# All work behind six transformer layers recast as ten stages that begin inside the layers' last four steps

## The chip, the cores and the metric

The kernel runs on one core of one Trainium2 chip. Its time is the device time of one execution in microseconds (us). TensorE is called PE, VectorE DVE, ScalarE ACT, GpSimd POOL and SyncE SP.

## What is computed

The input is `x`, 8 samples of 512 tokens with 128 channels, all in fp32. Four blocks follow one another, and each stands in `x = x + layernorm(block(layernorm(x)))`:

```python
# 1: six layers of linear attention with a feed-forward part (leaky relu)
for i in range(6):
    xn = _layernorm(x, ln1_w[i], ln1_b[i])
    q, k, v = xn @ wq[i], xn @ wk[i], xn @ wv[i]          # 8 heads of 16
    x = linear_attn(softmax(q, -1), softmax(k, -2), v) @ wo[i] + bo[i] + x
    xn = _layernorm(x, ln2_w[i], ln2_b[i])
    x = leaky_relu(xn @ w1[i]) @ w2[i] + x                # 128 -> 512 -> 128
# 2: spiking network
h = square(relu(x @ W_fc.T)); y = h @ W_proj.T            # 128 -> 512 -> 128
# five steps of a leaky integrator; the result is how often it fires / 5
# 3: state space model: u = x @ Win.T + bin; y = irfft(rfft(u) * rfft(k)) + u * D
y = y @ Wout.T + bout
# 4: gated channel mix with the token before
r = sigmoid(xr @ W_r.T); out = r * (square(relu(xk @ W_k.T)) @ W_v.T)
```

## The kernel before, in words

Each engine has one hand-written queue of instructions, with semaphores between them (`then_inc` where something is done, `wait_ge` where it is needed). A sample is 128 partitions x 512 columns, and nearly every instruction works on such a tile or on its four 128-column parts. An "item" is one sample in one layer, 48 in all (`ITEMS`). The program goes by steps: in step n every engine does some part of item n (attention), n-1 (the output projection), n-2 (second norm, `second_scale`, `second_turn`, `second_copy`, `second_low`) and n-3 (the feed-forward part, PE's `h` and `y`, ACT's `hl`). Steps 0 to 50 are the `layers` steps, and within each the order of an engine's instructions is the order of the lines in its function `step`.

The work behind the layers has stages of its own: ADD, PART, TURN, FFN, SPIKE, STATE, CONV, BACK, SHIFT, GATE, FINISH are numbered 0 to 10, and sample v is in stage k at step 48 + k + v. Steps 51 to 65 stand in a second function on each engine, `late_step`. The spiking network's first two matrix products go through the layers' own functions and buffers: its input is normalised with the layers' `STATS`, `JOIN` and `RSTD`, turned and split into a high and a low f32r part (`X2H`, `X2L`), and multiplied as three f32r matmuls (`split3`) with `FCH` and `FCL`. POOL's `join` and `ln1_power` serve both the layers and these samples.

What comes behind it is one chain for each sample: `count` adds five thresholded tiles on PE (`SPK`); four normalisations, each with DVE's `stats` (four `bn_stats`, four `bn_aggr`), POOL's `rstd` or `rstd_mean` (a power of -0.5 and two small products), ACT's `normalise` or `scaled` and POOL's addition to `X` (L778); `bands`, `transform`, `products`, `inverse`, `back_bands` and `project_out` for the convolution; `key_and_gate` and `value` for the last block. PSUM has eight banks, PS0 to PS7: `pXT`, `pQ`, `pK`, `pX2`, two of `pH`, `pY` and `pW`, and who writes one waits until the last reader is through.

In `late_step` PE does, in this order: `project_in`, the spiking products with `inverse` between them, `key_and_gate`, `second_turn`, `count`, `transform`, `value`, `project_out`, the turns. DVE has `products` at the very end of a step, and `inverse`, which needs them, comes in the next.

Of the kernel before, what the change touches and what calls it, by code (L numbers as in the profile page):

```python
# [13 lines left out]
P = 128  # L14
# [15 lines left out]
ALL = ITEMS + BATCH  # L30
# [54 lines left out]
def layers(step):  # L85

    for n in range(ITEMS + 3):
# [10 lines left out]
def live(n):  # L100

    return n < ITEMS, 1 <= n <= ITEMS, 2 <= n < ALL + 2, 3 <= n < ALL + 3

ADD, PART, TURN, FFN, SPIKE, STATE, CONV, BACK, SHIFT, GATE, FINISH = range(11)


def sample(n, stage):

    v = n - ITEMS - stage
    return v if 0 <= v < BATCH else None


def passed(n, stage):

    return max(0, min(BATCH, n - ITEMS - stage + 1))


def late(step):  # L120
    for n in range(ITEMS + 3, ITEMS + BATCH + FINISH):
        step(n)
# [3 lines left out]
DECAY = BATCH  # L126
# [4 lines left out]
SPECTRUM = {ITEMS: (0, 1, 2, 3), ITEMS + 1: (4, 5, 6, 7), ITEMS + 2: (8,)}  # L131
# [7 lines left out]
def build(nc, x, qkv, wo, w1, w2, lnc, bo, fcT, proj, winT, woutT, alog, bmat, cmat, dtr, dp, bins_,  # L139
          bouts, wrT, wkT, wvT, mu, ident, cent, hmask, iota, fwd, fwdx, inv, out):  # L140
    ctx = ExitStack()
    with ctx:  # L142
# [3 lines left out]
        def sem(name):  # L146
# [34 lines left out]
        MVS = [sb(f"MV{i}", [8]) for i in range(5)]  # L181
        STS = [sb(f"ST{i}", [24]) for i in range(5)]
        VES, RS, NMS = ([sb(f"{n}{i}", [4]) for i in range(5)] for n in ("VE", "R", "NM"))
# [21 lines left out]
        YM, ACC, MEM, U = QF, QB, EK, EKT  # L205
# [23 lines left out]

        PS = [ctx.enter_context(nc.psum_tensor(f"PS{i}", [P, SEQ], FP32)) for i in range(8)]  # L230
# [4 lines left out]
            "bias_out bias_ps bm_out bm_ps bo_c bo_mean bo_st c_in c_ps cdb ce1 ce1_zero ct e1 e1_arg e2 e2_arg eighth "  # L235
            "ek ekT_ps ek_tm fc_hi fc_out fc_ps g_ps gt h_ps hl i_rstd i_st i_var i_ve k_fm k_out k_ps k_rec k_skip "
            "kf kf_ps kmax ktm la la_exp late_in ln1_half ln1_rstd ln2_rstd ln_part m_ps m_ready mbv mixed out_ps p_const "
            "p_part q0_in q_blk q_exp q_fm q_nrm q_ps q_rec q_sub q_sum qmax qs relu resid1 resid2 sh0 ssm_in "
            "stats_ready stored v_part w1_hi w1_lo w2_c w2_mean w2_sum w_ready win_out win_ps wo_c wo_mean wo_st "
            "wqk_hi wqk_lo wv x2T_ps x2h x2l xT_ps xTh xTl xi_init xr xr2 y_ps "  # L240
            "added ym spk cnt_ps cnt_var cnt_nm cnt_z cnt_x st_var st_rstd st_x st_T_ps st_T u_ps u_sum "
            "bands f_ps f_part spectra inv_ps second back o_ps o_sum o_var o_nm o_z o_x sh_var "
            "sh_nm sh_z sh_T_ps sh_T r_ps k2_ps r_relu r_sq r_sig v_ps rv rv_var rv_nm rv_z done").split()
# [70 lines left out]
        def _(pe):  # L314
# [44 lines left out]
            def h(item, f):  # L359
                w = item // BATCH % 2  # L360
                if f == 0:
                    if item < ITEMS:
                        pe.wait_ge(s["w1_lo"], item // BATCH + 1)
                    else:
                        pe.wait_ge(s["fc_out"], 1)
# [4 lines left out]
                high, low = (W1H[w], W1L[w]) if item < ITEMS else (FCH, FCL)  # L370
                o = slice(f * P, (f + 1) * P)
                split3(pH[f % 2][:, :], high[:, o], low[:, o], X2H[:, :], X2L[:, :]).then_inc(s["h_ps"], 1)

            def y(item, f):
                w = item // BATCH % 2
                pe.wait_ge(s["hl"], item * FB + f + 1)
                if f == 0:
                    if item < ITEMS:
                        pe.wait_ge(s["w2_c"], item // BATCH + 1)
                    if some(item):  # L380
                        pe.wait_ge(s["resid2"], min(item, ITEMS))
                    if item > ITEMS:
                        pe.wait_ge(s["ym"], item - ITEMS)
# [1155 lines left out]
```

## Time and profile before

| what | value |
| --- | --- |
| median of 3 runs | 908.49 us (907.61 to 909.62) |
| the profiled execution's own time | 908.03 us |
| its span (first to last instruction) | 906.2 us |
| PE busy in the span | 810.6 us (89%) |
| DVE busy | 667.5 us (74%) |
| ACT busy | 588.1 us (65%) |
| POOL busy | 463.3 us (51%) |
| mean granted clock of PE | 0.962 of 2.4 GHz |

The profile's times are from the span's start. Busy times count instructions that run, not waits. A row of the timeline that holds several instructions of one kind gives the time from the start of the first to the end of the last; an fp32 matmul of PE stands there as two records, so x8 is four matmuls. A matmul's own duration overlaps with the next one, so what it costs in a row of them is the distance between starts.

### The profile page before, as it was taken

The page shows a single profiled execution, that of the slowest core. Times are in us where ns is not written, and L with a number is a line of the kernel's source. Part 1 is how long each engine was busy: PE and PEld are TensorE (multiplying, and loading weights), DVE is VectorE, ACT ScalarE, POOL GpSimd, SP SyncE. Part 2 cuts the span into 40 slices and gives each one's busy share as a digit, 9 for nine tenths or more (in the row PEclk, how much of TensorE's full clock was granted, in tenths as well). Part 3 has the DMA queues.
Part 4 walks back from the last instruction along what each step waited for, and adds up shares of the span by engine and source line. Part 5 has one row for each costly group of instructions (what it writes and reads, how often), then busy time and mean ns, then how long its engine had stood idle before and what let it go on. Part 6 is the DMA issues. An engine that isn't in the chain of part 4 may idle for free. (4 is left out here: it accounts for less than half of the span.)

```text
span 906.2 us, 15899 instructions
## 1 busy us (share of the span) xinstructions
PE 810.6 (89%) x5386; PEld 707.3 (78%) x5386; DVE 667.5 (74%) x1866; ACT 588.1 (65%) x1244; POOL 463.3 (51%) x772
## 2 busy tenths in 40 slices
PE   7689999999999999999999999999689888777674
PEld 3477888998999899999999988888578776656553
DVE  4687888878778887887888878874558877587741
ACT  3476777787778777777777777656655555533353
POOL 6888446565765554454544454443453435244333
PEclk9799999999999999999999999999979998999986
DMA  8200001000010001000100000000000000000001
GB/s 256 73 1 1 1 1 37 1 1 1 1 36 2 1 1 36 1 1 1 37 1 2 1 1 1 1 2 1 1 0 1 2 0 3 11 13 13 12 12 37
DMA packets 19728, 13.70 MB, mean 15 GB/s; under 512 B 2487, under 2 KB 18494, under 8 KB 19646
## 3 DMA queue, kind: packets, MB, share of 16 engines
q1 hardware_dynamic: 19646, 12.67, 4.8%
q8 instruction: 44, 0.72, 0.4%
q14 instruction: 38, 0.31, 0.1%
HBM read 10.57 MB, written 2.10 MB: 14 GB/s over the span
## 5 line engine op out<-in xcount | busy, mean ns | idle before, releaser
L316 PE MATMUL PS<-W,HL 128*128 128x128 f32 x1536 | 201.7, 275 | 0.0
L316 PEld LDWEIGHTS PS<-W,HL 128*128 128x128 f32 x1536 | 193.2, 191 | 8.2
L888 ACT ACTIVATE HL<-PS 128x512 f32<-128x512 f32 x192 | 109.3, 593 | 18.3 <-PE PS L316 14.0
L712 POOL TENSOR_TENSOR JOIN<-STATS 128x8 f32<-128x8 f32 (+1 forms) x56 | 14.6, 262 | 197.7 <-DVE STATS L1164 197.7
L316 PE MATMUL PS<-X2H,W1L 128*128 128x512 f32 x192 | 89.3, 465 | 6.3 <-issue 5.0
L874 ACT ACTIVATE XR<-XI,RSTD 128x128 f32<-128x128 f32 x224 | 71.7, 395 | 28.5 <-POOL RSTD L730 27.9
L960 ACT ACTIVATE EK<-PS,NKM 128x512 f32<-128x512 f32 x48 | 33.0, 688 | 81.8 <-DVE NKM L1284 81.8
L1164 DVE BATCH_NORM_STATS2 STATS<-XI 128x6 f32<-128x128 f32 x384 | 82.4, 277 | 1.6 <-POOL JOIN L713 1.5
L761 POOL TENSOR_TENSOR QB<-QB,QRC 128x512 f32<-128x512 f32 x48 | 50.9, 1059 | 61.3 <-DVE QRC L1316 61.3
L316 PE MATMUL PS<-X2L,W1H 128*128 128x512 f32 x192 | 76.1, 396 | 0.0
L316 PE MATMUL PS<-X2H,W1H 128*128 128x512 f32 x192 | 75.7, 394 | 0.0
L326 PE MATMUL PS<-ID,XR 128*128 128x128 f32 x416 | 64.9, 278 | 7.9 <-ACT XR L874 7.9
L656 POOL TENSOR_SCALAR VE<-MV 128x4 f32<-128x4 f32 x40 | 8.1, 203 | 120.7 <-DVE MV L1081 119.8
L730 POOL TENSOR_TENSOR RSTD<-JOIN,MHALF 128x4 f32<-128x4 f32 x48 | 64.1, 1336 | 0.0
L316 PE MATMUL PS<-MM,QS 128*128 128x128 f32 x384 | 55.6, 289 | 4.1 <-DVE MM L1269 2.8
L723 POOL TENSOR_TENSOR RSTD<-JOIN,MHALF 128x4 f32<-128x4 f32 x56 | 56.6, 1011 | 4.4
L1291 DVE STREAM_TRANSPOSE QB<-QF 128x512 f32<-128x512 f32 x48 | 34.1, 711 | 33.1 <-ACT QF L826 33.1
L326 PEld LDWEIGHTS PS<-ID,XR 128*128 128x128 f32 x416 | 47.1, 142 | 14.2 <-ACT XR L874 12.7
L1281 DVE TENSOR_TENSOR XI<-PS,XI 128x512 f32<-128x512 f32 x48 | 33.2, 692 | 30.6 <-PE PS L316 30.6
L316 PEld LDWEIGHTS PS<-MM,QS 128*128 128x128 f32 x384 | 48.2, 197 | 8.3 <-DVE MM L1269 5.7
L316 PE MATMUL PS<-EKT,XR 128*128 128x128 f32 x384 | 51.0, 276 | 1.6 <-ACT EKT L826 1.6
L316 PE MATMUL PS<-INV,BIG 128*128 128x256 f32 x128 | 38.7, 469 | 14.6 <-DVE BIG L1366 14.6
(214 smaller groups left out, 2189.4 us busy)
## 6 DMA issues: line engine op xcount, KB each, us to landing
W<-in_w SPq DMA_DIRECT2D x12, 256.0 KB
X<-in_x SPq DMA_DIRECT2D x8, 256.0 KB, 4.9
out<-X SPq DMA_DIRECT2D x8, 256.0 KB, 2.3
QKV<-in_qkv SPq DMA_DIRECT2D x6, 192.0 KB, 2.8
FWD<-in_fwd SPq DMA_DIRECT2D x1, 1024.0 KB, 5.5
INV<-in_inv SPq DMA_DIRECT2D x1, 1024.0 KB, 8.3
WO<-in_wo SPq DMA_DIRECT2D x6, 64.0 KB
FWDX<-in_fwdx SPq DMA_DIRECT2D x1, 256.0 KB, 5.9
```

What stands on the lines that cost most here:

```text
L316: return nc.tensor.matmul(o, l, r, start=start, stop=stop, skip_group_check=True)
L326: last = nc.tensor.transpose(o[:, j * P:(j + 1) * P], i[:, j * P:(j + 1) * P], ID[:, :])
L712: pool.tensor_tensor(d, part(1), part(4), ALU.subtract)
L723: pool.tensor_tensor(RSTD[:, TILES:end], JOIN[:, 4, TILES:end], MHALF[:, TILES:end], ALU.pow).then_inc(s["ln2_rstd"], 1)
L730: power = pool.tensor_tensor(RSTD[:, 0:TILES], variance, MHALF[:, 0:TILES], ALU.pow)
L761: pool.tensor_tensor(heads(QB[:, :]), heads(QB[:, :]), QRC[:, :].unsqueeze(2).broadcast_to([P, 32, DH]), ALU.mult).then_inc(s["q_nrm"], 1)
L874: last = nc.scalar.activation(o[:, j * P:(j + 1) * P], tile(src, b, j), ACT.Copy, scale=r[:, first + j:first + j + 1])
L888: nc.scalar.activation(HL[f][:, :], pH[f % 2][:, :], ACT.Prelu, alpha=LEAK).then_inc(s["hl"], 1)
L960: nc.scalar.activation(EK[:, :], pK[:, :], ACT.Exp, bias=NKM[:, 0:1], accum_out=KSM[:, 0:1]).then_inc(s["ek"], 1)
L1164: last = nc.vector.bn_stats(STATS[:, first + j, :], tile(src, b, j))
L1281: tt(xo, pQ[:, :], xo, ALU.add).then_inc(s["resid1"], 1)
L1291: nc.vector.transpose(QB[:, :], QF[:, :]).then_inc(s["q_blk"], 1)
```

## The change

`late_step` is gone on every engine, and with it the eleven stages and the samples' way through the layers' functions. All work behind the layers is written as some fifty small operations, each of which runs on one engine for one sample in one of ten stages; sample v is in stage k at step 44 + k + v (`FIRST` is 44). The last steps of the layers (44 to 50) and the steps behind them (to 60) are the same function `step`, in which each operation stands at a given place. There are 61 steps in place of 66.

```diff
-ALL = ITEMS + BATCH
+FIRST = ITEMS - 4
...
-ADD, PART, TURN, FFN, SPIKE, STATE, CONV, BACK, SHIFT, GATE, FINISH = range(11)
...
-    v = n - ITEMS - stage
+    v = n - FIRST - stage
...
+def at(n, stage, operation, *block):
+    v = sample(n, stage)
+    if v is not None:
+        operation(v, *block)
...
-DECAY = BATCH
+DECAY = BATCH - 2
...
+STEPS_IN_ALL = FIRST + BATCH + 9
...
-        FCH, FCL = sb("FCH", [FB * P], F32R), sb("FCL", [FB * P], F32R)
+        FCC = FCT
+        X2S, X2T = sb("X2S", [SEQ]), sb("X2T", [SEQ])
...
+        YM = W2[0]
...
+        ACTS = [HA[0], HA[1], W1[0], W1[1]]
...
+            def spiking_first(v, f):
+                pe.wait_ge(s["fc_out"], 1)
+                pe.wait_ge(s["in_T"], v + 1)
+                mm(pH[f % 2][:, :], FCC[:, f * P:(f + 1) * P], X2T[:, :]).then_inc(s["fh_ps"], 1)
...
+            def spiking_second(v, f):
+                pe.wait_ge(s["fhl"], v * FB + f + 1)
+                for j in range(TILES):
+                    last = mm(pW[:, j * P:(j + 1) * P], ACTS[f][:, j * P:(j + 1) * P],
...
+                if sample(n, 6) is not None:
+                    freed("resid1", min(n-1, ITEMS))
...
+                    transform(sample(n, 6), 1)
...
+                if sample(n, 5) is not None:
+                    freed("xTh", min(n+1, ITEMS))
+                    freed("ek_tm", min(n, ITEMS))
+                    freed("cnt_z", passed(n - 1, 3))
...
+                    project_in(sample(n, 5))
...
+                    inverse(sample(n, 6))
...
+            def left_add(v):
+
+                dve.wait_ge(s["fin_rstd"], v + 1)
+                for j in range(TILES):
+                    last = stt(out=tile(X, v, j), in0=tile(XI, v, j), scalar=RS[LEFT][:, j:j + 1], in1=tile(X, v, j),
+                               op0=ALU.mult, op1=ALU.add)
...
+                at(n, 7, output_stats)
+                at(n, 6, real_products)
+                at(n, 0, left_stats)
+                at(n, 6, imaginary_products)
+                at(n, 6, spectra)
+                at(n, 5, input_bias)
+                at(n, 4, state_stats)
```

The stages are: 0 the norm behind the layers and its addition (`left_stats`, `left_add`) and the norm's numbers of the spiking input (`spiking_stats`); 1 turn, the four first products and two of the four second ones; 2 the other two; 3 spikes and count; 4 the count's norm and addition, norm and turn for the state space model; 5 `project_in`, `bands`, the first half of `transform`; 6 its second half, the products, `inverse`, `back_bands`, `project_out`; 7 two norms, an addition and a turn; 8 key, gate, value; 9 the last norm and addition. The spiking input is fp32 now and has buffers of its own, so `split3` gives way to one fp32 matmul for each f; DVE's subtraction for `X2L` and POOL's `join` and `ln1_power` fall away for these samples. `DECAY` starts the preparation of the convolution's kernel two steps earlier.

PE, one full step in the middle of the late work, before. WINC is `project_in`, PROJ and HL the spiking network's second products, INV `inverse`, SH,WK the key, WR the gate, SPK the count, FWD `transform`, WVT `value`, WOUTT `project_out`, ID a turn:

```order
L316 MATMUL PS<-WINC,BIG 128x128 x4
...
L316 MATMUL PS<-INV,BIG 128x256 x8
L316 MATMUL PS<-PROJ,HL 128x128 x4
...
L316 MATMUL PS<-SH,WK 128x512 x2
L316 MATMUL PS<-WR,SH 128x128 x8
L316 MATMUL PS<-PROJ,HL 128x128 x4
...
L316 MATMUL PS<-SPK,IDB 128x512 x5
L316 MATMUL PS<-BIG,FWD 128x128 x16
L316 MATMUL PS<-WVT,BIG 128x128 x4
L316 MATMUL PS<-WOUTT,BIG 128x128 x4
```

The same place after the change (step 52; X2T,FCT are the spiking network's first products):

```order
L317 MATMUL PS<-WINC,BIG 128x128 x4
L317 MATMUL PS<-X2T,FCT 128x512
L317 MATMUL PS<-SH,WK 128x512 x2
L317 MATMUL PS<-INV,BIG 128x256 x8
L317 MATMUL PS<-X2T,FCT 128x512
L317 MATMUL PS<-PROJ,HA 128x128 x4
L317 MATMUL PS<-WR,SH 128x128 x8
L317 MATMUL PS<-X2T,FCT 128x512
L317 MATMUL PS<-WVT,BIG 128x128 x4
L317 MATMUL PS<-SPK,IDB 128x512 x5
L317 MATMUL PS<-X2T,FCT 128x512
L317 MATMUL PS<-PROJ,HA 128x128 x4
```

`transform` no longer stands in one piece: half of it comes at the step's end and half at the start of the next. `inverse` stays near the middle, and between any two operations that depend on each other others stand.

DVE in the same two steps. L1351 and L1375 are the spikes, L1431 and L1442 the bias behind `project_out`, L1359 to L1363 and L1405 to L1413 the four products. Before, the end of a step:

```order
L1424 TENSOR_TENSOR QB<-PS,BIG 128x512
L1078 BN_STATS ST<-QB 128x6 x4
L1081 BN_AGGR MV<-ST 128x2 x4
L1431 TENSOR_TENSOR BIG<-PS,BOUT 128x512
L1078 BN_STATS ST<-BIG 128x6 x4
L1081 BN_AGGR MV<-ST 128x2 x4
L1359 TENSOR_TENSOR BIG<-PS,KRE 128x512
L1360 TENSOR_TENSOR BIG<-PS,KIM 128x512
L1362 TENSOR_TENSOR BIG<-PS,KIM 128x512
L1363 TENSOR_TENSOR BIG<-PS,KRB 128x512
L1365 TENSOR_TENSOR BIG<-BIG 128x512
L1366 TENSOR_TENSOR BIG<-BIG 128x512
```

After, the start of a step:

```order
L1375 TENSOR_SCALAR SPK<-W 128x512 x5
L1442 TENSOR_TENSOR BIG<-PS,BOUT 128x512
L1194 BN_STATS ST<-BIG 128x6 x4
L1197 BN_AGGR MV<-ST 128x2 x4
L1405 TENSOR_TENSOR BIG<-PS,KRE 128x512
L1406 TENSOR_TENSOR BIG<-PS,KIM 128x512
L1412 TENSOR_TENSOR BIG<-PS,KIM 128x512
L1413 TENSOR_TENSOR BIG<-PS,KRB 128x512
L1418 TENSOR_TENSOR BIG<-BIG 128x512
L1419 TENSOR_TENSOR BIG<-BIG 128x512
L1391 TENSOR_TENSOR EKT<-PS,BIN 128x512
```

The spikes, which stood between `bands` and `back_bands`, now open the step; the products stand ahead of the wait for `project_in`, and DVE's other work of the step stands behind them, between the spectra and `back_bands`.

## Rows read from the trace of the kernel before

**Rows 1.** The page: span; busy time, share and instructions of each engine.

```profile
span 906.2 us, 15899 instructions
PE 810.6 (89%) x5386; PEld 707.3 (78%) x5386; DVE 667.5 (74%) x1866; ACT 588.1 (65%) x1244; POOL 463.3 (51%) x772
```

**Rows 2.** Two stretches: from:to, length, busy by engine, PE's clock, DMA share, GB/s.

```profile
200.00:500.00 300.00, 298.04 (x2153) 272.43 (x2152) 244.38 (x582) 226.76 (x469) 159.26 (x244) 1.00 0.03 9
700.00:860.00 160.00, 124.21 (x768) 106.16 (x766) 115.37 (x428) 76.26 (x173) 65.52 (x122) 0.93 0.03 8
```

**Rows 3.** Timeline of DVE: its last instruction in steps 24, 25 and 43.

```profile
322.40 0.63 DVE L1320 TENSOR_TENSOR XI<-PS,XI 128x512 f32<-128x512 f32 x1
334.27 0.63 DVE L1320 TENSOR_TENSOR XI<-PS,XI 128x512 f32<-128x512 f32 x1
...
551.06 0.63 DVE L1320 TENSOR_TENSOR XI<-PS,XI 128x512 f32<-128x512 f32 x1
```

**Rows 4.** Timelines of DVE and PE: the last sample's first product and its inverse.

```profile
858.28 0.66 DVE L1359 TENSOR_TENSOR BIG<-PS,KRE 128x512 f32<-128x512 f32 x1
862.12 6.43 PE L316 MATMUL PS<-INV,BIG 128*128 128x256 f32 x16 [5.36 <-DVE BIG L1366]
```

**Rows 5.** Timeline of PE in late steps: start, duration, line, names.

```profile
685.20 0.40 PE L316 MATMUL PS<-X2H,FCH 128*128 128x512 f32 x1
685.43 0.40 PE L316 MATMUL PS<-X2H,FCL 128*128 128x512 f32 x1
...
690.23 3.62 PE L316 MATMUL PS<-INV,BIG 128*128 128x256 f32 x16
...
742.62 1.88 PE L316 MATMUL PS<-SH,WK 128*128 128x512 f32 x4
...
748.40 1.24 PE L316 MATMUL PS<-SPK,IDB 128*128 128x512 bf16 x5
749.48 3.73 PE L316 MATMUL PS<-BIG,FWD 128*128 128x128 f32 x32
753.04 1.06 PE L316 MATMUL PS<-WVT,BIG 128*128 128x128 f32 x8
```

**Rows 6.** Timelines of DVE, of POOL and of ACT in late steps.

```profile
765.65 0.66 DVE L1339 TENSOR_TENSOR EKT<-PS,BIN 128x512 f32<-128x512 f32 x1
...
766.68 0.42 DVE L1177 TENSOR_TENSOR FLY<-EKT 128x256 f32<-128x256 f32 x1
...
768.07 1.28 DVE L1191 TENSOR_TENSOR BIG<-EKT,FLY 128x128 f32<-128x128 f32 x1
...
769.88 1.76 DVE L1351 TENSOR_SCALAR SPK<-QF 128x512 bf16<-128x512 f32 x5
771.75 0.42 DVE L1373 TENSOR_TENSOR YAC<-PS,YR 128x256 f32<-128x256 f32 x1
...
774.34 0.28 DVE L1382 SCALAR_TENSOR_TENSOR BIG<-YBC,YE 128x128 f32<-128x128 f32 x1
...
785.53 0.69 DVE L1431 TENSOR_TENSOR BIG<-PS,BOUT 128x512 f32<-128x512 f32 x1
...
787.46 0.66 DVE L1359 TENSOR_TENSOR BIG<-PS,KRE 128x512 f32<-128x512 f32 x1
...
789.95 0.69 DVE L1365 TENSOR_TENSOR BIG<-BIG 128x512 f32<-128x512 f32 x1
...
766.90 1.18 POOL L657 TENSOR_TENSOR R<-VE,MHALF 128x4 f32<-128x4 f32 x1
767.94 1.26 POOL L778 TENSOR_TENSOR X<-X,EK 128x512 f32<-128x512 f32 x1
...
785.62 0.19 POOL L656 TENSOR_SCALAR VE<-MV 128x4 f32<-128x4 f32 x1 [3.37 <-DVE MV L1081]
...
787.27 0.19 POOL L663 TENSOR_SCALAR NM<-NM 128x4 f32<-128x4 f32 x1
...
789.50 1.65 ACT L831 ACTIVATE BIG<-BIG,NM,R 128x128 f32<-128x128 f32 x4 [1.53 <-POOL NM L663]
```

More of the change, by code:

```diff
@@ new lines, in count, with state_turn, project_in @@
+            def count(v):
+                for t in range(STEPS):
+                    pe.wait_ge(s["spk"], v * STEPS + t + 1)
+                    last = mm(pXT[:, :], IDB[:, :], SPK[t][:, :], t == 0, t == STEPS - 1)
+                last.then_inc(s["cnt_ps"], 1)
+            def state_turn(v):
+                pe.wait_ge(s["st_x"], v + 1)
+                transposes(pX2, XS).then_inc(s["st_T_ps"], 1)
+            def project_in(v):
+                pe.wait_ge(s["win_out"], 1)
+                pe.wait_ge(s["st_T"], v + 1)
+                for j in range(TILES):
+                    last = mm(pXT[:, j * P:(j + 1) * P], XTS[:, j * P:(j + 1) * P], WINC[:, :])
+                last.then_inc(s["u_ps"], 1)
@@ new lines, in transform, with inverse @@
+            def transform(v, half):
+                pe.wait_ge(s["bands"], v + 1)
+                pe.wait_ge(s["kf"], 3)
+                bank = (pK, pQ)[half]
+                for k in range(TILES):
+                    for j in range(2):
+                        last = mm(bank[:, k * P:(k + 1) * P], FWD[:, j * BINS * P + half * SEQ + k * P:][:, 0:P],
+                                  V[:, (2 * k + j) * P:(2 * k + j + 1) * P], j == 0, j == 1)
+                last.then_inc(s["f_ps"], 1)
+            def inverse(v):
+                pe.wait_ge(s["spectra"], v + 1)
+                for block in (0, 2, 1, 3):
+                    bank = (pK, pQ)[block % 2]
+                    o = bank[:, (block // 2) * 2 * P:(block // 2 + 1) * 2 * P]
+                    for part in range(2):
+                        k = part * TILES + block
+                        last = mm(o, YF[:, k * P:(k + 1) * P], INV[:, k * 2 * P:(k + 1) * 2 * P], part == 0, part == 1)
+                last.then_inc(s["inv_ps"], 1)
@@ L531, in inverse @@
-            def inverse(v):
-                pe.wait_ge(s["spectra"], v + 1)
-                for block in (0, 2, 1, 3):
-                    bank = (pK, pW)[block % 2]
-                    o = bank[:, (block // 2) * 2 * P:(block // 2 + 1) * 2 * P]
-                    for part in range(2):
-                        k = part * TILES + block
-                        last = mm(o, YF[:, k * P:(k + 1) * P], INV[:, k * 2 * P:(k + 1) * 2 * P], part == 0, part == 1)
-                last.then_inc(s["inv_ps"], 1)
@@ new lines, in spiking_copy, with relu @@
+            def spiking_copy(v):
+                act.wait_ge(s["in_T_ps"], v + 1)
+                if some(v):
+                    act.wait_ge(s["fh_ps"], v * FB)
+                copy(X2T[:, :], pX2[:, :]).then_inc(s["in_T"], 1)
+            def relu(v, f):
+                act.wait_ge(s["fh_ps"], v * FB + f + 1)
+                if some(v):
+                    act.wait_ge(s["fy_ps"], v * FB + f - 3)
+                nc.scalar.activation(ACTS[f][:, :], pH[f % 2][:, :], ACT.Relu).then_inc(s["relu"], 1)
@@ new lines, in spiking_stats, with spikes @@
+            def spiking_stats(v):
+                dve.wait_ge(s["added"], v + 1)
+                if some(v):
+                    dve.wait_ge(s["in_rstd"], v)
+                stats(lambda j: tile(X, v, j), SPIKING).then_inc(s["in_var"], 1)
+            def spikes(v):
+                dve.wait_ge(s["ym"], v + 1)
+                if some(v):
+                    dve.wait_ge(s["cnt_ps"], v)
+                for t in range(STEPS):
+                    ts(SPK[t][:, :], YM[:, :], LEVELS[t], None, ALU.is_gt).then_inc(s["spk"], 1)
@@ L1288, in step @@
                     attention_weights(layer + 1)
+                at(n, 7, shift_stats)
+                at(n, 5, bands)
+                at(n, 6, back_bands)
+                at(n, 0, left_add)
                 if has_n:
```

896 lines of the change are left out of this document (454 added, 442 removed).

## The prediction, made before the changed kernel ran

> **What bounds the kernel now.** I read the page first [rows 1]: PE is busy 89% of a span of 906.2 us, DVE 74%. That share is a mean over two very different parts, so next come the windows [rows 2]. From 200 to 500 us PE is busy 298.0 of 300 us at the full clock: the layers are bound by PE, 11.87 us a step (334.27 - 322.40) [rows 3]. From 700 to 860 us PE is busy 124.2 of 160 us (78%), DVE 115.4 (72%), ACT 76.3 (48%) and POOL 65.5 (41%), and PE's mean clock is 0.93. No engine is full: there the order of the queues sets the time. The timeline shows one of its places: PE stood idle for 5.36 us ahead of `inverse`, for the spectra of `products` (L1366), which DVE makes at the end of its step although PE needs them early in the next; and `inverse` then ran at the low clock, 6.43 us [rows 4] for the 3.62 of another step [rows 5]. Step 43 ends with DVE's L1320 at 551.06 us [rows 3], so the 22 steps from 44 to the end take 906.2 - 551.6 = 354.6 us (I put the boundary at 551.6, when that instruction is through). This is what the change rewrites.
>
> **The change part by part.** First what one sample costs on PE at the full clock, as distances between starts [rows 5]. `transform` takes 753.04 - 749.48 = 3.56 for 16 matmuls, so 0.22 each for 128 fp32 columns. `inverse` 3.45 (its 3.62 less the overlap with the next). The key, 1.88 less the same overlap (3.73 - 3.56 = 0.17), 1.72 for two matmuls of 512 columns, 0.86 each. The gate 8 x 0.22 = 1.78, the count 749.48 - 748.40 = 1.08, value, `project_in` and `project_out` 0.89 each, the second spiking products 16 x 0.22 = 3.56, three turns about 0.45 each. The first spiking products were four times three f32r matmuls at 0.23 (685.43 - 685.20) [rows 5], 2.8 in all; the change makes them four fp32 matmuls of 512 columns, 3.44 at the key's 0.86. So this part of the change costs PE about 0.65 a sample; it removes a DVE subtraction (0.69) and POOL's `join`. The sum after the change is 22.6 us a sample.
>
> DVE for one sample [rows 6]: bias and `bands` 769.88 - 765.65 = 4.23, the five spikes 771.75 - 769.88 = 1.87, `back_bands` 774.62 - 771.75 = 2.87, the output bias with its statistics 787.46 - 785.53 = 1.93, so a set of statistics is 1.93 - 0.69 = 1.24 (1.28 with its semaphore). The four products take 789.95 - 787.46 = 2.49, the two spectra 1.3. Seven sets of statistics are 9.0; the gate's product 0.7; the output bias 0.7; `left_add` is new: four instructions on 128 columns, of the kind that closes `back_bands` at 0.28; I take 0.85 with their overlap, at least the 0.69 of one full tile and at most 4 x 0.28 = 1.1. Sum: 24.0 us. ACT comes to about 18 (six normalisations or scalings of up to 1.65, fourteen copies or squares of some 0.6) and POOL to about 16 (seven powers with what goes with them, 787.46 - 785.62 = 1.84 for the longer kind, and three additions of 1.26), both under DVE's sum.
>
> The layers' own rest: four full steps (44 to 47) of 11.87 on PE and 244.4/300 x 11.87 = 9.7 on DVE; steps 48, 49 and 50 still hold 7.7, 6.8 and 5.0 us of PE's work (the instructions of `step` for items already begun, at the distances above) and 5.0, 2.5 and 0.6 on DVE; the spectrum of the convolution's kernel 18 matmuls, 4.0.
>
> Now each step costs what its fuller engine has to do. In step 44 that is DVE: 9.7 + 3.4 (stage 0) + 1.9 (mixing of weights and first band additions), 15.0. PE in step 45: 11.9 + 5.7 (stage 1: turn, four first and two second products) = 17.5; step 46 adds stage 2 (1.78), 19.3; step 47 the count, 20.4; step 48 18.5; step 49 20.7; step 50, with `inverse` and the last layer work, 22.8. Step 51: DVE 22.0 (24.0 less the gated block's 2.0), PE 18.3. Step 52: PE 22.6, DVE 20.6. Steps 53 and 54: DVE 20.6 each, while PE falls to 17 and 15; 55: 17.4 (no spikes and no count); 56: 16.2. Sum over steps 44 to 56: 253.6 us.
>
> Whether the order lets the fuller engine run, I walked through three steps, each queue in its order, with these durations. In step 52 every operation of PE finds its input: `project_in` starts at 4.0 us and needs `pXT` back, which ACT's `count_norm` frees at 3.7; `inverse` at 7.5, its spectra are ready at 4.5 because the products now open DVE's step; `state_turn` ends at 22.7. In step 47 PE has 19.9 us of work and waits nowhere: `xTl`, the exponentials and `x2l` come 0.5 us or more before they are asked for. In step 54 DVE works without a gap. What is moved with it: on POOL the additions to `X` and the powers, each behind a wait of its own; on SP nothing, it issues the same eight output DMAs, each behind `done`. So the stall of before [rows 4] goes, and what is late next is nothing in PE's or DVE's full steps.
>
> Three additions. Switching between kinds of matmul costs PE something in the layers (my distances give 11.3 for the 11.87 of a step): 4 us for steps 45 to 52. DVE's L1191 took 1.28 us where L1382 of the same size takes 0.28 [rows 6], while POOL's L778 added a tile to `X`; three such additions a sample can each hold DVE up for up to 1.0: 24 us at most, nothing at least, and I take 4, since only steps 51 and 53 to 56 are DVE's and one hold a step is in my `bands` already. And 1.2 us in steps 41 to 43, which now hold the kernel's copies and the centring that stood in 43 to 45.
>
> On that hold the Trainium skill has a rule (SBUF — State Buffer, section Who interferes with whom): a DVE instruction with two SBUF inputs and a GpSimd instruction that reads SBUF exclude one another. By it POOL's seven short powers a sample would hold DVE up as well, some 31 us more in the DVE-bound steps, a span near 891. The rows speak against that half: L1177, two SBUF inputs, took its 0.42 us under the power of 766.90 [rows 6]. So the sum goes by the additions alone.
>
> Then the drain. From step 57 only chains are left: output statistics 2.0, the products, `inverse`, `back_bands` and `project_out` of the last sample, two norms (power on POOL, normalisation on ACT, addition on POOL), turn, key, value, norm, addition, store. Walked link by link it is 15.0 us to the end of `project_out`, 13.9 more to the copy behind the shift's turn, 6.4 to the gate's statistics, and 7.6 for power, normalisation, addition and store: 43 us at the full clock, and 46 with PE at the low clock after its waits. The same chain before, from the last sample's first product at 858.28 to 906.2, took 48 us [rows 4]; mine from that product is 44.
>
> Sum: 551.6 + 1.2 + 253.6 + 4 + 4 + 46 = 860.4 us of span. The profiled execution took 908.03 for a span of 906.2, 1.8 more, and the median of the runs is 0.5 above it: 862.2 profiled, **863** as a median. A change of under 0.2% (1.8 us) can hardly be told from none here.
>
> **The rivals.**
> *(a) Part of the waits stay.* PE and DVE lean on ACT and POOL at some 20 places in a step, and I walked only three steps of thirteen. If the fuller engine is busy 88% of steps 44 to 56, they take 253.6/0.88 = 288, 35 more: 890 or so with the rest. The same time, some 893, comes out if each of POOL's powers holds DVE up by its 1.0 us as the additions do (seven a step in steps 51 and 53 to 56, about 31 us), for which no row here speaks. For (a) speaks the margin of 0.3 us at `project_in`; against it, that the other margins are over 0.5, and that PE reaches 99% in the layers with queues of the same kind [rows 2].
> *(b) Slower than before: the ring through `pXT`.* The count now lies in the bank that the layers' turns, `project_in` and the gate share, and is held until `count_norm` is through: statistics 1.3, POOL's four small instructions 1.84 (behind `gated_norm` and `spiking_rstd` in its queue), ACT's normalisation 1.65 [rows 6]. `project_in` waits for it at the head of PE's queue, with `inverse` and the spiking products behind. If this is late by 5.4 us a step, as long as PE's wait of before [rows 4], nine steps (48 to 56) lose 48 and the time is about 911. It decides from 5 us a step: 863 + 9 x 5 = 908. In step 52 I find it in time.
> *(c) The steps need not wait for one another.* Over steps 44 to 56 PE has 232 us and DVE 222 to do, both under the 253.6; where one engine's surplus in a step fills the other's next, 6 to 12 us go, and the time is 850 to 857.
> *(d) No gain:* the late work put into steps 44 to 47 slows these by as much as it saves behind. PE is full there, so each such instruction does lengthen the step; but it leaves steps in which PE was busy 78%, and this would need PE no fuller than before after the layers.
>
> **How the numbers follow.** My forecast, 855 to 878: 0.57. (a), up to 900: 0.18. (c), below 855: 0.12. (b): 0.08. (d), within 0.2%: 0.02. The remaining 0.03 is a mix between (a) and no change. The range leaves out (b), (d), the upper third of (a) and the end of (c): 847 to 890. Faster 0.89, same 0.02, slower 0.09.
>
> **What would show it.** Step 44 should begin near 553, and the layers' last addition (`resid2` of step 50) end near 690. PE should be busy over 93% of the stretch from 553 to 690 at the full clock; DVE over 93% from about 712 to 810. PE's wait for the spectra should be gone up to step 55. The drain, from the last sample's first product, should be 44 us. I am wrong if PE shows waits of over 1 us for ACT's normalisations or copies in steps 45 to 52 (then (a) or (b)), if DVE's two-input instructions show 1 us more than their 0.28 or 0.69 many times a step (then the hold was under-priced), or if the fp32 first products take other than 0.86 apart.

## The result, and the profile after

The changed kernel takes **846.47 us** (median of 4 runs, 844.96 to 846.93) against 908.12 for the kernel before beside it: a ratio of 0.9332, 95% interval 0.9315 to 0.9349, so 61.7 us less. The profiled execution took 846.16 us for a span of 844.3. The predicted 863 was 16.5 too high. The time missed the forecast proper (855 to 878) and lies at the very low end of the whole range (847 to 890): 0.5 us below it as a median, and just inside it, at 847.8, as the ratio times the 908.49 that the prediction started from. The direction was right, and so was the mechanism. In the experiments below, three single executions (4441 and 2754 us of the kernel before, 1258 us of the one with one f32r pass) took far longer than all others of their kernels and are left out of the ratios.

The page of the changed kernel, against [rows 1]:

```profile
span 844.3 us, 16194 instructions
PE 791.0 (94%) x5354; PEld 687.8 (81%) x5354; DVE 662.4 (78%) x1937; ACT 584.7 (69%) x1244; POOL 462.1 (55%) x740
PEclk9799999999999999999999999999999999999996
DMA  9200000100000000100001000000000000000001
```

The engines have hardly less to do: PE 791.0 us for 810.6 (19.6 less, with the mean granted clock at 0.981 for 0.962), DVE 662.4 for 667.5. Of the 61.9 us by which the span is shorter, 42.3 are time in which PE stood idle, and 19.6 are PE's busy time, most of it because fewer matmuls run at the low clock behind a wait.

Five stretches of the changed kernel (from:to, length, busy by engine PE, PEld, DVE, ACT, POOL, PE's clock, DMA share, GB/s), against [rows 2]:

```profile
200.00:500.00 300.00, 298.34 (x2153) 272.59 (x2151) 244.04 (x582) 225.75 (x466) 156.81 (x242) 1.00 0.03 9
553.00:690.00 137.00, 134.54 (x905) 114.73 (x904) 106.57 (x388) 96.89 (x209) 58.05 (x100) 0.99 0.01 1
700.00:800.00 100.00, 91.84 (x617) 77.58 (x616) 94.16 (x372) 62.03 (x148) 58.53 (x99) 0.98 0.04 12
712.00:810.00 98.00, 88.69 (x577) 74.25 (x576) 88.66 (x345) 57.55 (x138) 58.72 (x98) 0.98 0.04 12
780.00:844.30 64.30, 42.14 (x255) 34.26 (x254) 35.00 (x136) 28.23 (x65) 28.79 (x52) 0.88 0.07 21
```

The layers are as before. From 553 to 690 us PE is busy 98% at the full clock. From 700 to 800 DVE is busy 94% and PE 92%, where before it was 72% and 78%, at a mean clock of 0.98 for 0.93. Only the last 46 us are a chain with idle engines.

The place of [rows 4] and [rows 5], on PE's timeline of the changed kernel in step 51 (start, duration, line, names):

```profile
691.47 1.02 PE L317 MATMUL PS<-X2T,FCT 128*128 128x512 f32 x2
692.57 3.69 PE L317 MATMUL PS<-INV,BIG 128*128 128x256 f32 x16
696.10 1.02 PE L317 MATMUL PS<-X2T,FCT 128*128 128x512 f32 x2
696.96 1.05 PE L317 MATMUL PS<-PROJ,HA 128*128 128x128 f32 x8
697.85 1.02 PE L317 MATMUL PS<-X2T,FCT 128*128 128x512 f32 x2
698.71 1.24 PE L317 MATMUL PS<-SPK,IDB 128*128 128x512 bf16 x5
699.79 1.02 PE L317 MATMUL PS<-X2T,FCT 128*128 128x512 f32 x2
700.64 0.61 PE L317 MATMUL PS<-PROJ,HA 128*128 128x128 f32 x4
```

`inverse` follows without a wait and takes 3.69 us. The fp32 first product costs 0.86 between starts (696.10 to 696.96). The first such wait is late: 1.33 us in step 56, when most stages are empty. The second row is the last sample's, which is the one that [rows 4] shows for the kernel before: 1.15 us of waiting and 3.69 of work for 5.36 and 6.43.

```profile
788.72 3.69 PE L317 MATMUL PS<-INV,BIG 128*128 128x256 f32 x16 [1.33 <-DVE BIG L1419]
...
804.47 3.69 PE L317 MATMUL PS<-INV,BIG 128*128 128x256 f32 x16 [1.15 <-DVE BIG L1419]
```

[rows 4] was the largest wait of its kind, not a typical one. Two of PE's waits in the kernel before from 660 to 880 us (who waited for whom, us in total, times, longest):

```profile
PE PS L316 <- DVE BIG L1366: 14.6, 4, 5.4
PE PS L316 <- ACT HL L893: 12.7, 5, 4.1
```

Three samples before the last waited 3.1 us for the spectra and the samples before those not at all; ACT's tiles between the spiking products (`HL`) held PE up nearly as long. In the changed kernel both are gone from the full steps.

The ends of the sum, on DVE's timeline of the changed kernel. The first row is where step 44 begins, the second the layers' last addition (`resid2`), the third where step 51 begins, the last the final sample's first product:

```profile
552.80 1.23 DVE L1315 TENSOR_TENSOR XR<-XI,RSTD 128x512 f32<-128x512 f32 x1
...
680.82 0.69 DVE L1544 TENSOR_TENSOR XI<-PS,XI 128x512 f32<-128x512 f32 x1
...
683.12 1.73 DVE L1375 TENSOR_SCALAR SPK<-W 128x512 bf16<-128x512 f32 x5
...
799.99 0.66 DVE L1405 TENSOR_TENSOR BIG<-PS,KRE 128x512 f32<-128x512 f32 x1
```

(Step 51 begins behind that addition with the spikes.)

### The profile page after: what moved, and what is told of

Read it like the earlier page. It is cut to its first block, busy times and chain, and to the rows that moved or that the text cites. A ratio compares the mean times of both kernels' runs of the same rounds, so it can differ in the third digit from the quotient of the medians.

```text
span 844.3 us, 16194 instructions
## 1 busy us (share of the span) xinstructions
PE 791.0 (94%) x5354; PEld 687.8 (81%) x5354; DVE 662.4 (78%) x1937; ACT 584.7 (69%) x1244; POOL 462.1 (55%) x740
## 4 chain that ended last, share of the span: by engine, by line
PE 76%; POOL 9%; DVE 7%; issue 4%; ACT 3%; DMA 0%; POOLq 0%; ACTq 0%; DVEq 0%
PE PS L317 68%; PE PS L327 8%; POOL XI L767 2%; ACT BIG L913 1%; POOL QB L877 1%; POOL RSTD L790 1%; POOL RSTD L797 1%; POOL RX L758 1%; ACT XR L956 1%; DVE QSM L1537 1%; DVE STATS L1273 1%; DVE STX L1258 1%; POOL R L725 1%; DVE ST L1194 0%; DVE XR L1315 0%
## 5 line engine op out<-in xcount | busy, mean ns | idle before, releaser
L779 POOL TENSOR_TENSOR JOIN<-STATS 128x8 f32<-128x8 f32 (+1 forms) x48 | 12.2, 254 | 159.0 <-DVE STATS L1273 159.0
L956 ACT ACTIVATE XR<-XI,RSTD 128x128 f32<-128x128 f32 x192 | 61.5, 393 | 25.4 <-POOL RSTD L797 25.3
L1273 DVE BATCH_NORM_STATS2 STATS<-XI 128x6 f32<-128x128 f32 x352 | 75.5, 277 | 0.1
L327 PE MATMUL PS<-ID,XR 128*128 128x128 f32 x384 | 61.2, 283 | 9.4 <-ACT XR L956 9.4
L724 POOL TENSOR_SCALAR VE<-MV 128x4 f32<-128x4 f32 x56 | 13.5, 241 | 102.8 <-DVE MV L1197 101.4
L725 POOL TENSOR_TENSOR R<-VE,MHALF 128x4 f32<-128x4 f32 x56 | 59.8, 1069 | 4.7
L327 PEld LDWEIGHTS PS<-ID,XR 128*128 128x128 f32 x384 | 44.4, 144 | 15.1 <-ACT XR L956 12.4
L797 POOL TENSOR_TENSOR RSTD<-JOIN,MHALF 128x4 f32<-128x4 f32 x40 | 55.2, 1381 | 0.0
L877 POOL TENSOR_TENSOR QB<-QB,QMX 128x512 f32<-128x512 f32 x48 | 51.7, 1078 | 4.5 <-DVE QMX L1513 4.5
L1320 DVE TENSOR_TENSOR X2L<-X2F,X2H 128x512 fp32r<-128x512 f32 x48 | 36.0, 749 | 23.2 <-ACT X2F L961 23.1
```

The costliest lines, as they stand in the source:

```text
L327: last = nc.tensor.transpose(o[:, j * P:(j + 1) * P], i[:, j * P:(j + 1) * P], ID[:, :])
L725: return pool.tensor_tensor(RS[k][:, :], VES[k][:, :], MHALF[:, 0:TILES], ALU.pow)
L797: power = pool.tensor_tensor(RSTD[:, 0:TILES], variance, MHALF[:, 0:TILES], ALU.pow)
L877: pool.tensor_tensor(heads(QB[:, :]), heads(QB[:, :]), QMX[:, :].unsqueeze(2).broadcast_to([P, 32, DH]), ALU.subtract).then_inc(s["q_sub"], 1)
L956: last = nc.scalar.activation(o[:, j * P:(j + 1) * P], tile(src, b, j), ACT.Copy, scale=r[:, first + j:first + j + 1])
L1273: last = nc.vector.bn_stats(STATS[:, first + j, :], tile(src, b, j))
```

## The experiments

Each ran beside the kernel before on the same chip, and the ratios are to that. The last column is the difference of a kernel's ratio from 0.9332, times 908.1 us: what it costs (+) or saves (-) against the changed kernel. Differences of less than some 3 us are within the intervals.

| kernel | us | ratio (95% interval) | against changed |
| --- | --- | --- | --- |
| stages begin at step 48 | 858.81 | 0.9472 (0.9442 to 0.9501) | +12.7 |
| stages begin at step 50 | 862.98 | 0.9524 (0.9500 to 0.9548) | +17.4 |
| the same, queues in the old order | 918.71 | 1.0143 (1.0117 to 1.0169) | +73.6 |
| products and transform last | 880.64 | 0.9716 (0.9689 to 0.9743) | +34.9 |
| transform alone in one piece | 850.25 | 0.9377 (0.9358 to 0.9396) | +4.1 |
| first products in one f32r pass | 831.16 | 0.9167 (0.9133 to 0.9202) | -15.0 |
| one more tile on DVE | 851.33 | 0.9383 (0.9352 to 0.9415) | +4.6 |
| one more tile on ACT | 846.57 | 0.9338 (0.9308 to 0.9367) | +0.5 |
| split first products, subtraction first | 857.34 | 0.9464 (0.9439 to 0.9489) | +12.0 |
| the same, behind one product | 853.57 | 0.9423 (0.9398 to 0.9448) | +8.3 |
| the same, behind the spectra | 849.18 | 0.9348 (0.9330 to 0.9366) | +1.5 |

The theory was: the gain comes from the order, which lets the fuller engine of each step work without a gap (W), and to a small part from beginning early. The rivals were that the early beginning (O), the buffers or other waits gave it.

**How much does the early beginning give?**

```diff
-FIRST = ITEMS - 4
+FIRST = ITEMS
```

> The changed kernel with the ten stages beginning in step 48 in place of 44 (65 steps in place of 61), nothing else. Theory W (the work of the fuller of PE and DVE sets each step): PE's total is the same, the layers' steps 44 to 47 shrink to 12 to 13 us, and the later ones hold less; summed as in the prediction the end moves by 0 to +8 us, 846 to 855. Rival O (the gain comes from laying late work over the layers' last four steps): four more steps of 17 to 20 us replace four of 12.5, 18 to 30 us slower, 865 to 877.

It costs 12.7 us to begin at step 48, above what W gave (up to 8) and below what O gave (18 and more): the early beginning is worth about a fifth of the gain, and the rest has another source. A second kernel begins at step 50 (`ITEMS + 2`), the layers' last, and serves as control for the one after it:

> The changed kernel with its stages beginning in step 50: almost nothing of the late work lies over the layers. It is the control for the next run. The stages in step 48 cost 12.3 us more than in step 44; two steps later again, with steps 49 to 52 nearly empty, I expect 5 to 9 us more: 864 to 868.

It costs 4.7 us more than beginning at step 48, where I expected 5 to 9.

**The order alone.** Operations, buffers and PSUM banks are those of the control, but in `step` of PE, DVE, ACT and POOL the late operations stand as `late_step` had them (where one moves past a step's end, its stage number moves by one). An extract of DVE's part; PE's `transform` is in one piece again too:

```diff
-                at(n, 3, spikes)
...
-                at(n, 7, output_stats)
-                at(n, 6, real_products)
-                at(n, 0, left_stats)
-                at(n, 6, imaginary_products)
-                at(n, 6, spectra)
-                at(n, 5, input_bias)
-                at(n, 4, state_stats)
...
-                at(n, 5, bands)
-                at(n, 6, back_bands)
...
+                at(n, 5, input_bias)
+                at(n, 5, bands)
+                at(n, 3, spikes)
+                at(n, 6, back_bands)
...
+                at(n, 6, output_stats)
+                at(n, 5, real_products)
+                at(n, 5, imaginary_products)
+                at(n, 5, spectra)
```

> As the control with stages from step 50 and with all operations, buffers and banks of the changed kernel, but the operations behind the layers stand on PE, DVE, ACT and POOL in the order of the kernel before (spiking products of two steps around inverse, transform in one piece at the end, products last on DVE, normalisations where they stood). Theory Q (the order of the queues is what made the late steps long): 895 to 912, 30 us or more above the control. Rival B (own buffers, no join and no shared RSTD, one fp32 matmul in place of three f32r): the order costs little, 866 to 878.

It was 56 us slower than the control (1.0143 - 0.9524, times 908.1), more than either theory said (Q gave up to 912). The same stretch of both kernels, first the control, then the old order:

```profile
700.00:800.00 100.00, 91.86 (x619) 77.38 (x618) 94.84 (x383) 64.80 (x155) 63.51 (x106) 1.00 0.03 9
```

```profile
700.00:800.00 100.00, 83.66 (x507) 67.31 (x505) 72.28 (x279) 54.16 (x123) 36.90 (x70) 0.93 0.01 4
```

DVE falls from 95% to 72%, the figure of the kernel before [rows 2], PE does 505 to 507 matmul records in 100 us for 619, and the clock is 0.93 again. Two of its waits, on PE's and DVE's timelines:

```profile
719.28 1.66 PE L317 MATMUL PS<-X2T,FCT 128*128 128x512 f32 x2 [4.32 <-ACT HA L943]
```

```profile
737.20 0.69 DVE L1368 TENSOR_TENSOR BIG<-PS,BOUT 128x512 f32<-128x512 f32 x1 [3.89 <-PE PS L317]
```

So the account closes in three steps: new operations and buffers in the old order +13.0 us against the kernel before, the order -56.2, beginning six steps earlier -17.4. What makes up the 13 was not taken apart. The kernel with the old order ends its last sample one step later than the kernel before (in step 66, not 65), its first products are fp32, and its PSUM banks were laid out for the new order. By this last point a part of the 56 may belong to the old order's meeting banks that do not suit it; no run has the old banks in the new order.

**Which move matters?** The products are put back at the end of DVE's step, and the transform whole at the end of PE's:

```diff
-                if sample(n, 6) is not None:
...
-                    transform(sample(n, 6), 1)
...
                     transform(sample(n, 5), 0)
...
+                    transform(sample(n, 5), 1)
...
                 at(n, 7, output_stats)
-                at(n, 6, real_products)
                 at(n, 0, left_stats)
-                at(n, 6, imaginary_products)
-                at(n, 6, spectra)
...
                 at(n, 3, count_stats)
+                at(n, 5, real_products)
+                at(n, 5, imaginary_products)
+                at(n, 5, spectra)
```

> The changed kernel with one place undone: both halves of transform at the end of PE's step, and the four products and the spectra at the end of DVE's step, ahead of inverse in the next, as before the change. If the wait for the spectra that the prediction named was a large part of the old loss: 12 us or more above the changed kernel, 858 and more. If it only showed where the chain of a whole step ended: PE has 5.5 us of other work ahead of inverse, 0 to 4 us more, 846 to 850.

34.9 us: more than half of the order's worth hangs on this place, far more than I had expected of it. And it does not lie where I looked. DVE's timeline in step 52 of this kernel:

```profile
712.49 0.68 DVE L1418 TENSOR_TENSOR BIG<-BIG 128x512 f32<-128x512 f32 x1
713.09 1.76 DVE L1374 TENSOR_SCALAR SPK<-W 128x512 bf16<-128x512 f32 x5
714.77 0.68 DVE L1441 TENSOR_TENSOR BIG<-PS,BOUT 128x512 f32<-128x512 f32 x1
715.48 0.87 DVE L1193 BATCH_NORM_STATS2 ST<-BIG 128x6 f32<-128x128 f32 x4
716.39 0.38 DVE L1196 BATCH_NORM_AGGREGATE MV<-ST 128x2 f32<-128x6 f32 x4
716.68 0.66 DVE L1390 TENSOR_TENSOR EKT<-PS,BIN 128x512 f32<-128x512 f32 x1
719.95 0.87 DVE L1193 BATCH_NORM_STATS2 ST<-X 128x6 f32<-128x128 f32 x4 [2.61 <-POOL X L832]
...
733.27 0.69 DVE L1404 TENSOR_TENSOR BIG<-PS,KRE 128x512 f32<-128x512 f32 x1 [1.83 <-PE PS L317]
...
735.05 0.69 DVE L1411 TENSOR_TENSOR BIG<-PS,KIM 128x512 f32<-128x512 f32 x1 [0.50 <-PE PS L317]
```

The spectra are ready in time, so `inverse` has no wait. But now nothing but the input bias stands between the output statistics (715.48) and the statistics of `X` that need POOL's power, ACT's normalisation and POOL's addition first: DVE idles 2.61 us. In the changed kernel the products fill that place. And at the other end of the step (733.27 and 735.05) the products now wait for the transform that PE finishes just ahead of them, 1.83 and 0.50 us, where in the changed kernel it is 0.15 us at most in steps 51 to 55. With 0.51 at 721.75, for the next addition to `X`, these waits come to 5.5 us, and a step grew by 4 to 5. PE is then late in its turn, 1.05 to 1.07 us at a time on ACT's tiles, and each step takes 24 to 25 us in place of 20. Half of the edit alone, PE's part, with DVE's order left as in the changed kernel:

```diff
-                if sample(n, 6) is not None:
...
-                    transform(sample(n, 6), 1)
...
                     transform(sample(n, 5), 0)
...
+                    transform(sample(n, 5), 1)
```

> Half of the run with the products last: only TensorE's order is changed. The transform's second half (eight matmuls into pQ) follows the first half directly at the end of TensorE's step, where in the changed kernel it opens the next step. VectorE's order is that of the changed kernel (output_stats, then the products and spectra, early in the next step). Theory O (the 34 us that the products-last run lost against the changed kernel came from VectorE's order: output_stats, spikes and what follows them were pushed back by the products): this run stays within 3 us of the changed kernel, 845 to 850. Rival T (TensorE's transform in one piece holds up the other products at the step's end): at least half of the loss is here, 863 or more. Between 850 and 863 both take part.

+4.1 us, a little over what O allowed and far from T: some 31 of the 35 us come only when DVE's order is changed as well.

**Which engine sets the time?** Three kernels change the work of one engine. The first makes the four first products of each sample one f32r pass; it leaves out the low parts, so its values are rounded to the f32r format:

```diff
-        FCC = FCT
-        X2S, X2T = sb("X2S", [SEQ]), sb("X2T", [SEQ])
+        FCC = sb("FCC", [FB * P], F32R)
+        X2S, X2T = sb("X2S", [SEQ]), sb("X2T", [SEQ], F32R)
```

> The spiking network's four first products per sample read f32r tiles (weights and input rounded by ACT), so PE needs one f32r pass, some 0.23 us, instead of an fp32 matmul of 0.86; the rounding changes the values, and the low parts are left out. It takes 2.5 us of PE a sample away and nothing else. Theory W: PE is the fuller engine in steps 45 to 50, so six times 2.5 us go, and step 52 is DVE's: 15 us less, 829 to 834. Rival C (chains through ACT and POOL set the steps): 0 to 5 us less.

The others add one full tile for each sample, into a buffer that nobody reads: on DVE in `output_stats` (steps 51 to 58), on ACT behind `output_norm`.

```diff
                 dve.wait_ge(s["o_sum"], v + 1)
+                tt(XR2[:, :], YO[:, :], ID[:, 0:1].broadcast_to([P, SEQ]), ALU.mult)
```

> One more VectorE multiplication of a full tile (0.67 us, a scratch result that nobody reads) in each sample's output statistics, steps 51 to 58. Theory W: DVE is the fuller engine in steps 51 to 56 and on the path in the drain, so 4 to 5 us more, 850 to 852. Rival C: hidden in DVE's waits, under 1.5 us.

```diff
                 normalise(ZOUT[:, :], YO[:, :], RS[OUTPUT], NMS[OUTPUT]).then_inc(s["o_z"], 1)
+                copy(XR2[:, :], QF[:, :])
```

> One more ScalarE copy of a full tile (0.6 us, a scratch result) behind each sample's output normalisation, steps 51 to 58. Theory W: ACT has slack, under 1 us more. Rival C: the chains run through ACT, so 3 to 5 us more, as much as for the same work on DVE.

PE's 20 us less (8 samples, 4 x (0.86 - 0.23) each, in steps 45 to 52) give 15.0; DVE's 5.5 more (8 x 0.69) cost 4.6; ACT's 4.9 (8 x 0.61) cost nothing that can be told. All three came out as W said. Work on PE counts at 74%. For DVE the share is rough, since its 4.6 carries some 3 us of uncertainty, but the kernels with a tile on DVE and on ACT ran side by side, and every execution of the first (848.75 and more) was slower than every one of the second (848.53 and less).

**The split kept, with buffers of its own.** The first products as three f32r matmuls, as before, and DVE's subtraction for the low part at three places in its queue. (To make room, two tiles share the space of others whose work is done: `X2S` that of `FCT`, `WINC` that of `IOTA`.) The diff is the first; in the second kernel the call stands behind `real_products`, in the third behind `spectra`:

```diff
-                mm(pH[f % 2][:, :], FCC[:, f * P:(f + 1) * P], X2T[:, :]).then_inc(s["fh_ps"], 1)
+                o = slice(f * P, (f + 1) * P)
+                split3(pH[f % 2][:, :], FCH[:, o], FCL[:, o], X2T[:, :], X2TL[:, :]).then_inc(s["fh_ps"], 1)
...
+            def spiking_low(v):
+                dve.wait_ge(s["in_h"], v + 1)
+                tt(X2TL[:, :], pX2[:, :], X2T[:, :].bitcast(FP32), ALU.subtract).then_inc(s["in_T"], 1)
...
                 at(n, 7, output_stats)
+                at(n, 1, spiking_low)
                 at(n, 6, real_products)
                 at(n, 0, left_stats)
                 at(n, 6, imaginary_products)
                 at(n, 6, spectra)
```

> The changed kernel with the first spiking products back as three f32r matmuls of high and low parts (in own buffers; DVE makes the low part from PSUM, 0.69 us a sample, steps 45 to 52). By the sums PE loses 0.65 us a sample in the PE-bound steps 45 to 50, 4 us less, and DVE gains 0.69 in 51 and 52, 1.4 more: 842 to 845. If the added link of the chain (turn, copy, low part, product) counts: 847 to 852.

> The three f32r matmuls of the split instead of one fp32 matmul in the spiking network's first products, as before, but with VectorE's subtraction that makes the low part one place later in its queue, behind the first product of the convolution instead of ahead of it. Theory P (place: in the earlier run VectorE stood 7.3 us and less in this wait with the products and spectra queued behind it, so the loss of 11 us against the changed kernel came from where the wait stands): the time comes down by at least 4 us, to 846 to 853. Rival L (the link itself: one more hand-over between ScalarE's copy and TensorE's first product costs wherever it stands): 855 to 860, no better than before.

> The split of the spiking network's first products again, with VectorE's subtraction for the low part behind the whole convolution part (both products and the spectra) of its queue. In the run before, with it behind the first product, VectorE waited 2.39 us in step 51 for ScalarE's copy, the spectra came behind that, and TensorE idled 3.85 us before the inverse transform, whose 16 matmuls then took 5.38 us where they take 3.69. Theory P (the loss lies in what stands behind the wait): the copy is done by the time that the spectra are, VectorE no longer waits, TensorE's idle time before the inverse goes below 1 us, the steps 50 and 51 come back to about 23 and 22 us, and the time is 845 to 849, within 3 us of the changed kernel. Rival L (the link costs wherever it stands): 852 to 860. TensorE may now wait up to 1 us for the subtraction before its first product; if that is 2 us or more, the wait has only moved, and the time stays above 850.

The first was slower than the sum allowed, and its move by one place gave 3.7 us: it left place and link undecided. Its trace named the mechanism, on DVE's and PE's timelines of that second kernel, step 51:

```profile
692.94 0.69 DVE L1377 TENSOR_TENSOR X2TL<-PS,X2T 128x512 fp32r<-128x512 f32 x1 [2.39 <-ACT X2T L910]
```

```profile
698.61 5.38 PE L318 MATMUL PS<-INV,BIG 128*128 128x256 f32 x16 [3.85 <-DVE BIG L1428]
```

DVE waits 2.39 us for ACT's copy, the spectra stand behind it (the second of them, pushed into POOL's addition, took 1.75 us for 0.68 as well), and PE idles 3.85 us ahead of `inverse`: the stall of [rows 4] is back, in the new order. In the third kernel neither row has a wait, the steps 50 and 51 take 22.3 and 21.5 us, and PE instead waits for the subtraction:

```profile
712.15 0.76 PE L318 MATMUL PS<-X2T,FCL 128*128 128x512 f32 x1 [2.52 <-DVE X2TL L1377]
```

That is over the 2 us at which I had said that the wait has only moved. Only step 52 shows one so long; shorter ones of 0.84, 1.13 and 1.55 us stand in steps 45, 48 and 51. The time still came down by 6.8 us to within 1.5 of the changed kernel. So the place of one instruction of 0.69 us moves the time by 10.5 us. The 12.0, 8.3 and 1.5 are the cost of the whole split, not of this instruction: its three f32r matmuls take PE 0.69 for the 0.86 of one fp32 matmul, which by the sum in its expectation saves 4 us.

## Why the prediction was right, and where its sum was off

**The bound and the stall.** Right. The layers are unchanged; the wait ahead of `inverse` [rows 4] is gone until step 56, and in the kernel with the old order it is back, 3.29 us in three steps and 5.52 in the last: so it was the order that removed it. It was one loss among several in the full steps, as the waits above show: the sum over each engine, not this one place, carried the prediction.

**The start.** 552.8 us was predicted for step 44 (551.6 + 1.2) and read: 552.80.

**Steps 44 to 56.** Predicted 253.6, and 4 + 4 on top; measured 798.1 - 552.8 = 245.3, from step marks on DVE (552.8, 567.2, 584.7, 603.5, 623.8, 641.0, 659.9, 683.1, 704.6, 725.0, 744.4, 763.9, 780.8, 798.1). This is the term that was mis-sized, by 16.3 us, the whole miss. By parts: step 44 14.4 for 15.0; steps 45 to 50, PE's, 115.9 for 119.2 + 4; steps 51 to 56, DVE's, 115.0 for 119.4 + 4.
- *Switching, 4 us.* Not there. PE was busy 134.54 of 137 us, and its steps came out at the distances between starts alone, or below. In step 49 (18.9 for 20.7) I had also counted the transform's first half (1.78), which PE does only at 660.84, behind DVE's mark; 1.5 us are still too much over the six steps. What the layers' 0.57 a step is (11.87 for 11.3), from which I took the allowance, was not taken apart.
- *The additions' hold on DVE, 4 us and the 1.0 within `bands`.* Mis-sized. POOL's addition to `X` no longer falls into `bands` but onto the spectra: over the eight samples L1418 takes 0.69 to 1.67 us, 3.1 us in all above its own 0.69, and L1419 once 1.1 above its own, so 4.2 us where my sum held 8 x 1.0 and 4 more. `bands` opens at 715.49 and ends at 718.00, 2.5 us for the 3.6 of [rows 6]. From step 50 on no step has more than one DVE instruction that is held up by 0.3 us or more. `left_add`, which I had at 0.85 and at most 1.1, takes 1.13 (L1360).
- *The fuller engine sets the step.* Right in its main part (the three kernels that shift work), but rival (c) took place too: in step 51 DVE has 22.0 us to do by my sum and the step took 21.5, in step 52 PE 22.6 and it took 20.4, since the surplus of one step is worked off in its neighbour. PE's own marks show that the durations were right and the rule was not: the transform's second half, which opens its step, starts at 663.77, 686.56, 705.09, 727.95 and 745.43, so PE's steps 50 to 53 took 22.8, 18.5, 22.9 and 17.5 us for the 22.8, 18.3, 22.6 and 17 of my sum. Adding up the fuller engine of each step charges both surpluses. I had given this 6 to 12 us, 850 to 857, and a chance of 0.12; with the two terms above it makes the time that came.

**The drain.** Predicted 44 us from the last sample's first product, measured 844.3 - 800.0 = 44.3; 46 from step 57, measured 46.2.

**The rest of what would show it.** PE over 93% busy from 553 to 690: 98%. DVE over 93% from 712 to 810: 90%, so this sign failed, since the last steps in it are half empty; 94% from 700 to 800. `resid2` ending near 690: 681.5, early by what the steps ahead of it were over-priced. The waits of (a) are few: in steps 45 to 52 PE has one, 0.25 us for ACT's `X2T` in step 48 (the 1.40 us in PE's own issue at 564.53 belong to step 44). The fp32 distance of 0.86 held.

**The rivals.** (a) fell: only steps 50 and 56 took more than their sums, by 0.4 and 1.1 us. (b) was right in kind and wrong in price. In steps 51 and 52 PE finds `pXT` free, as I had walked it; in steps 54 and 55 the ring closes, on ACT's and PE's timelines:

```profile
747.58 1.51 ACT L913 ACTIVATE BIG<-PS,NM,R 128x128 f32<-128x128 f32 x4 [1.36 <-POOL NM L731]
```

```profile
749.29 1.20 PE L317 MATMUL PS<-WINC,BIG 128*128 128x128 f32 x8 [1.92 <-issue]
```

`project_in` starts 0.2 us behind `count_norm` (747.58 + 1.51 = 749.09), after 1.92 us of idling, for which the profile names no releaser. These are 1.9 and 1.5 us in two steps, where (b) had 5.4 in nine. They cost nothing that can be seen: DVE sets these steps, and works through them with 0.2 us of waiting in step 54 and 0.5 in step 55. So that walk was right for DVE and said too little of PE. (d) fell, but had a point: beginning at step 44 instead of 48 gives 12.7 us where four steps fewer of some 20 would give 80; most of that work only lengthens PE's full steps.

## What to carry to other kernels

With in-order queues, first sum each engine's work per step. Here no engine was full (78% and 72%), and the order was what cost: reordering the same instructions was worth 56 us of 919. An instruction that waits costs what stands behind it, not its own length: put it behind work that others wait for, and put independent work between the two ends of a round trip through other engines (statistics, power, normalisation, addition; or the transform on PE and the products on DVE). Then make the sum with distances between starts alone: the allowance for switching was not needed here. Let neighbouring steps share their surplus, for adding up the fuller engine of each step gave too much.

## What the runs showed of the hardware

DVE and POOL exclude one another, in both directions but not for every instruction. DVE's and POOL's timelines of the changed kernel around two places:

```profile
667.15 1.67 DVE L1418 TENSOR_TENSOR BIG<-BIG 128x512 f32<-128x512 f32 x1
...
716.46 0.28 DVE L1292 TENSOR_TENSOR BIG<-FLY 128x128 f32<-128x128 f32 x1
716.66 0.28 DVE L1293 TENSOR_TENSOR BIG<-FLY 128x128 f32<-128x128 f32 x1
```

```profile
666.99 1.27 POOL L833 TENSOR_TENSOR X<-X,BIG 128x512 f32<-128x512 f32 x1 [4.71 <-ACT BIG L913]
668.35 0.52 POOL L724 TENSOR_SCALAR VE<-MV 128x4 f32<-128x4 f32 x1
...
711.99 1.75 POOL L849 TENSOR_TENSOR X<-X,BIG 128x512 f32<-128x512 f32 x1 [0.53 <-ACT BIG L913]
...
716.35 1.05 POOL L725 TENSOR_TENSOR R<-VE,MHALF 128x4 f32<-128x4 f32 x1
```

L1418 starts 0.16 us into POOL's addition and ends 0.56 us behind it, for 0.69 of its own: nearly all of its work came behind the addition. The other way round POOL's addition takes 1.75 us instead of 1.27 when it starts within DVE's two-input L1419 (711.93), and the small L724 0.52 instead of 0.20. But two DVE instructions with two SBUF inputs lie wholly within POOL's power of 128 x 4 (716.35 to 717.40) and take their 0.28; sixteen do so in this trace, at 0.28 to 0.29 each. The powers around them take 1.05 to 1.18 us, where most take 1.01 or 1.02. The Trainium skill (SBUF — State Buffer, section Who interferes with whom) has the exclusion, and that the one that comes first goes first; the trace agrees for the tile-sized additions (1.67 for 0.69), not for the power. The row on which the prediction set the rule aside, L1177 beside the power of 766.90 [rows 6], was badly chosen: DVE had begun first there. The conclusion held.

A stall can also slow what comes after it. In the second kernel with the split, `inverse` behind 3.85 us of idling took 5.38 us where it takes 3.69. The granted clock from 692 to 698, in which PE was busy 2.77 of 6 us, was 1.00; from 698.6 to 704, with PE busy throughout, it was 0.68, a mean of its two levels, 1.2 and 2.4 GHz:

```profile
692.00:698.00 6.00, 2.77 (x22) 2.28 (x20) 4.92 (x13) 4.04 (x9) 4.19 (x4) 1.00 0.01 3
698.60:704.00 5.40, 5.39 (x17) 4.48 (x18) 5.20 (x27) 0.00 (x0) 3.23 (x6) 0.68 0.00 0
```

So 1.69 us were added to a wait of 3.85. It does not follow every time: in the kernel with the old order `inverse` waited 3.29 us in three steps and then took 5.20, 3.69 and 5.38. The one of the three that kept the full clock:

```profile
827.34 3.69 PE L317 MATMUL PS<-INV,BIG 128*128 128x256 f32 x16 [3.29 <-DVE BIG L1345]
```

That kernel's mean clock from 700 to 800 us, 0.93 for the control's 1.00, has such places in it, as the 1.66 us behind the 4.32 of waiting at 719.28, for a pair that takes 1.02 elsewhere.
